# A graph network's last stage: keys and values first, queries behind them in groups of four tiles, biases from a broadcast row, one program block

## Chip, cores and metric

The kernel runs on one core of a Trainium2 chip. The metric is the device time of one execution in microseconds (us); lower is better. A core has five engines with an instruction stream each: TensorE (PE in the profile), VectorE (DVE), ScalarE (ACT), GpSimd (POOL) and SyncE (SP, which here only starts transfers).

## What is computed

The input is 3125 nodes with 128 features and 53125 edges sorted by destination node. Four graph layers follow one another, each with a residual and a layer norm. Three of them sum gathered rows over edges. The fourth, which the change touches with what stands just before it, is an attention over each node's edges:

```python
# h: [3125, 128] after three layers; row = dst, col = src of the edges; 8 heads of 16
x3 = layernorm(x2 + relu(agg @ W.T + b))          # end of layer 3
q = (h @ Wq + bq).reshape(n, 16, 8) * 16 ** -0.5  # h is x3
k = (h @ Wk + bk).reshape(n, 16, 8)
v = (h @ Wv + bv).reshape(n, 16, 8)
s = einsum('edh,edh->eh', q[row], k[col])
p = exp(s - segment_max(s, row)[row])
out = segment_sum(p / segment_sum(p, row)[row] * v[col], row)
```

## The kernel before

Nodes are held in 25 tiles of 128 (`NT`), edges in 416 chunks of 128 (`EC`). Every wait is written by hand: an instruction adds to a semaphore and another engine waits for a count. Each engine works off its own list in order.

The program has two parts, each a block of its own with a meeting of all engines behind it. The first, `sum_layers`, runs three passes over the chunks (the three sum layers), and then a `post_body`, called the bridge below. Each pass gathers its chunks one after another by indirect transfers that POOL issues (L507). At the end of a pass every engine adds one to `s_end`; DVE waits for all four, clears the pass's semaphores and lets the others go on with `s_go` (`pass_end` L371, `pass_close` L1163).

The bridge works tile by tile, in a software pipeline over `i`. For tile t, PE multiplies the summed rows by the layer's weight (`last_product`, L651) and adds the bias by a second, three-row bf16 product (L652); DVE adds the residual and takes the layer norm (`last_front` L1124, L977, L983; `last_back` L987, L1132); PE transposes the normalised tile (L658) and ACT copies it out of PSUM (L728). PE then makes queries, keys and values in one product 384 columns wide (`qkv`, L666) with the bias again as a second product (L667). ACT copies out of PSUM the scaled queries twice, as f32 and as bf16 (L737, L738), and keys and values as f32 (L740). Queries are stored as three bf16 parts whose sum is the f32 value, so DVE takes two differences (`rest`, L1143) and ACT two more casts (`part`, L744) for each tile. SP stores keys and values to `kv_d` in DRAM (L470, three buffers `kv_s`) and queries to `q_d` (L473, six buffers `q_s`). Between them DVE builds tables of penalties for the attention: seven operations at i = 8 (`row_tables`, L1100 to L1110) and 13 pairs from i = 14 (`chunk_tables`, L1116 and L1118). Their data comes by 16 transfers that POOL starts at the head of the bridge into the buffer `G` (L518).

The second part, `attention`, works in 26 steps of 16 chunks, called batches k, each of four quads q (four chunks). POOL gathers the rows of `kv_d` by chunk into `G2` (printed as `G`), a ring of 64 chunks (L1338); before every eighth chunk it waits until the values in that place are used. DVE first clears its buffers, and ACT rewrites the cleared sums (L1536). Then for every quad PE picks out the query rows (L1359, copied out by ACT in L1490, and L1369 into `p_qe`), and DVE multiplies them with the gathered keys (`products`, L1609) and sums by head (L1615). Once in a batch the scores are transposed (PE L1415, into `p_sT`), scanned for segment maxima (DVE L1626), exponentiated on ACT, and turned back. DVE then multiplies values by weights (`values`, L1676, into `PV`), and PE sums them into windows (L1406, L1409, into `p_w`). In most steps one tile of nodes is finished as well: PE L1427, DVE L1709 to L1720, ACT L1531. In `k`'s step DVE runs `products(4k-1)`, `products(4k)`, `products(4k+1)` and `products(4k+2)`, and the step ends with `values(4k-4)` and `values(4k-3)`.

## Time and profile before

| | us |
|---|---|
| median of 3 runs | 2334.08 (2333.65 to 2336.39) |
| the profiled execution | 2332.2 |
| its span | 2330.3 |
| three passes over the chunks | 0 to 1639 |
| the bridge, from its first operation to its last issue of a store | 1639.2 to 1720.2 |
| attention's gathers, first to last start | 1728.6 to 2286.4 |

The busy shares over the span are PE 72%, POOL 70%, DVE 66% and ACT 19%. They are averages over stages that have different limits, so each stage is read from its own rows. The granted TensorE clock was 0.50 of full speed (1.2 GHz) from 1650 to 1700 us, where the bridge runs, and 0.50 from 1750 us on.

### The profile page before, as it was taken

What the parts mean: (1) busy time and instruction counts of PE and PEld (TensorE: products, weight loads), DVE (VectorE), ACT (ScalarE), POOL (GpSimd) and SP (SyncE); (2) the same over time, 40 slices, a digit from 0 to 9 for tenths busy, and PEclk for the clock granted to TensorE, in tenths of its full rate; (3) what the DMA queues carried; (4) which work ended last, traced back from release to release, by engine and by line L of the source; (5) the groups of instructions that cost most, each with busy time, mean ns of one, the idle gap of its engine ahead of it and who ended that gap; (6) DMA issues with size and microseconds to landing.
All of it is one profiled execution on the core that took longest, in us unless ns stands there. A gap on an engine that the chain in (4) does not pass through costs nothing. (4 is left out here: it accounts for less than half of the span.)

```text
span 2330.3 us, 32319 instructions
## 1 busy us (share of the span) xinstructions
PE 1670.3 (72%) x8464; PEld 1238.1 (53%) x8464; DVE 1539.0 (66%) x5260; ACT 435.6 (19%) x994; POOL 1636.8 (70%) x1687
## 2 busy tenths in 40 slices
PE   4877777765766766775567667667957888888886
PEld 3655555553555555554444444444426667677775
DVE  8776776665666666664355555556657787788785
ACT  0000000002000000002111111111343343344342
POOL 6777777775777777775777777774227777777772
PEclk9975555555556665555587777787555555555555
DMA  5233233232233233235232332332423333333331
GB/s 139 56 85 83 57 85 84 56 84 70 56 84 84 85 84 112 56 84 155 54 98 83 98 99 83 98 99 82 80 87 107 105 108 106 108 105 107 108 104 36
DMA packets 149656, 207.12 MB, mean 89 GB/s; under 512 B 48936, under 2 KB 111387, under 8 KB 149360
## 3 DMA queue, kind: packets, MB, share of 16 engines
q0 software_dynamic: 61280, 138.20, 22.1%
q1 hardware_dynamic: 87186, 65.12, 9.5%
q10 hardware_dynamic: 1010, 1.73, 0.2%
q8 instruction: 73, 1.20, 0.2%
q14 instruction: 107, 0.88, 0.1%
HBM read 172.14 MB, written 36.04 MB: 89 GB/s over the span
## 5 line engine op out<-in xcount | busy, mean ns | idle before, releaser
L507 POOL DMA_INDIRECT G<-h_d,idx x832 | 794.6, 955 | 283.9 <-issue 261.8
L570 PE MATMUL p_g<-S,G 128*128 128x96 f32 (+1 forms) x2496 | 609.0, 390 | 462.6 <-DMA G<-h_d,idx 300.7
L570 PEld LDWEIGHTS p_g<-S,G 128*128 128x128 f32 x2496 | 526.6, 292 | 667.2 <-issue 295.0
L1338 POOL DMA_INDIRECT G<-kv_d,idx x416 | 432.4, 1039 | 201.8 <-issue 201.8
L507 POOL DMA_INDIRECT G<-in_x,idx x416 | 397.6, 956 | 132.2 <-issue 119.4
L928 DVE TENSOR_SCALAR work<-iota_h,key_f 128x600 bf16<-128x600 f16 x416 | 171.0, 411 | 253.9 <-PE p_d L581 253.6
L903 DVE SCALAR_TENSOR_TENSOR S<-con,rel,shared 128x96 f32<-128x96 f32 (+1 forms) x1248 | 315.4, 293 | 0.5
L581 PE MATMUL p_d<-work 128*128 128x312 bf16 (+1 forms) x832 | 272.2, 428 | 18.0 <-DVE work L943 17.1
L921 DVE TENSOR_TENSOR agg<-agg,p_g 128x96 f32 (+1 forms) x624 | 143.7, 230 | 104.1 <-PE p_g L570 84.3
L1406 PE MATMUL p_w<-S,PV 128*128 128x40 f32 x832 | 199.2, 415 | 0.7 <-DVE PV L1676 0.7
L943 DVE TENSOR_TENSOR work<-work,p_d 128x312 f32 (+1 forms) x416 | 190.8, 459 | 10.4 <-issue 9.6
L1406 PEld LDWEIGHTS p_w<-S,PV 128*128 128x128 f32 x832 | 186.6, 329 | 15.9 <-issue 10.8
L1019 DVE TENSOR_TENSOR work<-work,p_d 128x512 f32<-128x512 f32 (+1 forms) x168 | 104.3, 625 | 137.1 <-PE p_d L616 136.6
L616 PE MATMUL p_d<-work,q_s 128*128 128x512 bf16 (+1 forms) x525 | 161.0, 429 | 1.9 <-DVE q_s L1008 0.9
L581 PEld LDWEIGHTS p_d<-work 128*128 128x128 bf16 x832 | 116.6, 163 | 34.8 <-DVE work L929 18.1
L1359 PE MATMUL p_oh<-idb,ohn 128*120 128x128 bf16 x416 | 68.9, 321 | 75.8 <-ACT ohn L1483 43.0
L1615 DVE TENSOR_REDUCE hs<-XH 128x32 f32<-128x512 f32 x104 | 111.6, 1073 | 3.5
L705 ACT ACTIVATE xt_s<-p_xt 128x128 f32<-128x128 f32 x75 | 20.8, 278 | 488.8 <-PE p_xt L592 488.8
L929 DVE TENSOR_SCALAR work<-iota_h,lo_f 128x128 bf16<-128x128 f16 x416 | 109.6, 263 | 0.0
L1359 PEld LDWEIGHTS p_oh<-idb,ohn 128*120 128x120 bf16 x416 | 51.9, 213 | 93.0 <-ACT ohn L1483 56.6
L1609 DVE TENSOR_TENSOR XH<-p_qe,G 128x512 f32<-128x512 f32 x104 | 70.8, 681 | 45.7 <-DMA G<-kv_d,idx 35.6
L1676 DVE TENSOR_TENSOR PV<-G,ps 128x512 f32<-128x512 f32 x104 | 68.9, 684 | 20.8 <-PE p_w L1409 20.8
(253 smaller groups left out, 2093.3 us busy)
## 6 DMA issues: line engine op xcount, KB each, us to landing
work<-A_d SPq DMA_DIRECT2D x25, 800.0 KB, 4.5
A_d<-work SPq DMA_DIRECT2D x12, 1600.0 KB, 7.5
G<-h_d,idx POOLq DMA_INDIRECT x832, 2.5
G<-in_x,idx POOLq DMA_INDIRECT x416, 2.5
G<-kv_d,idx POOLq DMA_INDIRECT x416, 2.8
h_d<-XH SPq DMA_DIRECT2D x75, 64.0 KB
h_d<-in_x SPq DMA_DIRECT2D x2, 1600.0 KB, 7.4
kv_d<-kv_s SPq DMA_DIRECT2D x25, 128.0 KB, 1.7
```

What stands on the lines that cost most here:

```text
L507: pool.indirect_dma_start(G[:, c % GRING, :], None, l.table, bass.IndirectOffsetOnAxis(ap=l.places[:, c:c + 1], axis=0)).then_inc(s_arr[g ...
L570: last = pe.matmul(p_g[:, g % PB, 0:width], G[:, c % GRING, :], S[:, c % (SRING * GR), 0:width], start=(k == 0), stop=(k == GR - 1))
L581: last = pe.matmul(p_d[:, 1 + half, 0:(hi - lo) * W], lows[:, slot, :], keys[:, slot, lo * W:hi * W], start=(k == 0), stop=(k == GR - 1))
L616: last = pe.matmul(p_d[:, n % 3, 0:width], q_s[:, t % QS, k, :], A_s[:, t % AB, cols], start=(k == 0), stop=(k == QR - 1))
L903: last = dve.scalar_tensor_tensor(S[:, slot + k, 0:l.nb * W].rearrange("p (b w) -> p b w", w=W), bc(iota, 1, l.nb), rel[:, c:c + 1], bc(co ...
L921: dve.tensor_tensor(place, place, p_g[:, g % PB, 0:l.nb * W].rearrange("p (b w) -> p b w", w=W), ALU.add).then_inc(s_added, 1)
L928: dve.tensor_scalar(keys[:, slot, :], iota_h[:], key_f[:, c:c + 1], None, ALU.is_equal)
L943: dve.tensor_tensor(place, place, p_d[:, 1 + half, 0:(hi - lo) * W].rearrange("p (t w) -> p t w", w=W), ALU.add).then_inc(s_bad, 1)
L1338: pool.indirect_dma_start(G[:, c % KRING, :], None, d["kv"], bass.IndirectOffsetOnAxis(ap=idx[:, c:c + 1], axis=0)).then_inc(s_ar[c // QC ...
L1359: last = pe.matmul(p_oh[0:QR * WA, c * P:(c + 1) * P], ohn[:, k % 2, j * QC + c, :], idb[:], start=True, stop=True)
L1406: pe.matmul(p_w[:, q % 2, 0:WA], PV[:, q % 2, c, :], S01[:, j * QC + c, :], start=(c == 0), stop=(c == QC - 1))
L1615: dve.tensor_reduce(hs[:, j * QC:(j + 1) * QC, :], prod[:, j * QC:(j + 1) * QC, :].rearrange("p c (d h) -> p c h d", h=HEADS), AX_X, ALU.a ...
```

## The change

- Keys and values are made on their own, 256 columns wide. DVE takes them out of PSUM and adds the bias, which lies as a row broadcast over all partitions (`b_all`). The two bias products are gone, and the bias split that made their operands.
- The transposed tiles are kept in `H`. When all keys and values are done, PE makes the queries out of them, four tiles in one PSUM bank (seven groups, the last of one tile). DVE scales and adds the bias, and the three parts are made for four tiles at once; a store takes one group.
- The seven row tables are spread over i = 3 to 9, and the chunk tables begin at i = 10 instead of 14.
- There is one block instead of two. POOL does not meet the others at the end of the bridge: it waits for the stores of keys and values and for the tables, adds its one to `s_end`, and starts on attention's gathers. `agg` and `G` are placed first, so that `G2` lies over these two alone.

The diff without its changes of indentation (all four engine functions are moved from the blocks into plain functions); "..." marks what is left out:

```diff
-QS = 6
+QS = 3
+QG = 4
+QGROUPS = math.ceil(NT / QG)
...
+            def _(pool):
+                sums.gpsimd(pool)
+                att.gpsimd(pool)
...
+            def _(dve):
+                att.vector(dve, sums.vector(dve))
...
@@ SP @@
             def post_body():
-                for i in range(NT + 4):
-                    if i < NT:
-                        sp.wait_ge(s_kv, i + 1)
-                        sp.dma_start(d["kv"][i * P:(i + 1) * P, :], kv_s[:, i % 3, :]).then_inc(s_kvst[i % 3], 16)
-                    if (t := i - 4) >= 0:
-                        sp.wait_ge(s_q[4], t + 1)
-                        sp.dma_start(d["q"][t * P:(t + 1) * P, :],
-                                     q_s[:, t % QS].rearrange("p s d -> p (s d)")).then_inc(s_qst[t % QS], 16)
+            for t in range(NT):
+                sp.wait_ge(s_kv, t + 1)
+                sp.dma_start(d["kv"][t * P:(t + 1) * P, :], kv_s[:, t % 3, :]).then_inc(s_kvst[t % 3], 16)
+            for g in range(QGROUPS):
...
+                sp.wait_ge(s_q[5], g + 1)
+                sp.dma_start(rows, q_p[:, g % 3, 0:n].rearrange("p t s d -> p t (s d)")).then_inc(s_qst[g % 3], 16)
...
@@ POOL @@
             post_body()
-            pass_end(pool, turn)
+        for k in range(3):
+            pool.wait_ge(s_kvst[k], 16 * len(range(k, NT, 3)))
+        pool.wait_ge(s_tab, 7 + KB)
+        pool.sem_inc(s_end, 1)
...
@@ PE @@
             def last_product(t):
-                pe.matmul(p_g[:, t % 3, 0:D], aggT[:, t * P:(t + 1) * P], w_lin[:], start=True, stop=False)
-                pe.matmul(p_g[:, t % 3, 0:D], one_three[:], b_three[:, 0:D], start=False, stop=True).then_inc(s_o, 1)
+            pe.matmul(p_g[:, t % 3, 0:D], aggT[:, t * P:(t + 1) * P], w_lin[:], start=True, stop=True).then_inc(s_o, 1)
...
-                pe.matmul(p_d[:, t % 3, 0:3 * D], xt_s[:, t % 2, :], w_qkv[:], start=True, stop=False)
-                pe.matmul(p_d[:, t % 3, 0:3 * D], one_three[:], b_three[:, D:4 * D], start=False,
-                          stop=True).then_inc(s_qkv, 1)
+            pe.matmul(p_d[:, t % 3, 0:2 * D], H[:, t, :], w_qkv[:, D:3 * D], start=True, stop=True).then_inc(s_pkv, 1)
+
+        def queries(g):
+            if g < 3:
+                pe.wait_ge(s_kv, NT - 2 + g)
+            else:
+                pe.wait_ge(s_q[0], g - 2)
+            for j in range(min(QG, NT - g * QG)):
+                last = pe.matmul(p_d[:, (NT + g) % 3, j * D:(j + 1) * D], H[:, g * QG + j, :], w_qkv[:, 0:D],
+                                 start=True, stop=True)
+            last.then_inc(s_pq, 1)
...
@@ ACT @@
+        def part(g, k):
+            n = min(QG, NT - g * QG)
+            act.wait_ge(s_q[2 * k], g + 1)
...
+            act.activation(q_p[:, g % 3, 0:n, k, :], q_f[:, g % 3, 0:n, :], ACT.Copy).then_inc(s_q[2 * k + 1], 1)
...
@@ DVE @@
             def last_front(t):
-                dve.scalar_tensor_tensor(y[:, t % 2, :], p_g[:, t % 3, 0:D], 0.0, XA[:, t, :], ALU.max,
-                                         ALU.add).then_inc(s_y, 1)
+            dve.tensor_tensor(y[:, t % 2, :], p_g[:, t % 3, 0:D], b_lin, ALU.add).then_inc(s_y0, 1)
+            dve.wait_ge(s_y0, t + 1)
+            dve.scalar_tensor_tensor(y[:, t % 2, :], y[:, t % 2, :], 0.0, XA[:, t, :], ALU.max, ALU.add).then_inc(s_y, 1)
...
+        def keys_values(t):
+            dve.wait_ge(s_pkv, t + 1)
+            if t >= 3:
+                dve.wait_ge(s_kvst[t % 3], 16 * (t // 3))
+            dve.tensor_tensor(kv_s[:, t % 3, :], p_d[:, t % 3, 0:2 * D], b_kv, ALU.add).then_inc(s_kv, 1)
+
+        def scaled(g):
...
+            dve.scalar_tensor_tensor(q_f[:, g % 3, 0:n, :], p_d[:, (NT + g) % 3, 0:n * D].rearrange("p (t d) -> p t d", d=D),
+                                     float(HD) ** -0.5, bc(b_q, 1, n), ALU.mult, ALU.add).then_inc(s_q[0], 1)
...
+            dve.tensor_tensor(part, part, q_p[:, g % 3, 0:n, k - 1, :], ALU.subtract).then_inc(s_q[2 * k], 1)
...
             def post_body():
-                for i in range(NT + 6):
+            for i in range(NT + 4):
...
+                    keys_values(i - 4)
+                if 3 <= i < 10:
+                    row_tables(i - 3)
+                if 10 <= i < 10 + KB // 2:
+                    chunk_tables(i - 10)
+            dve.wait_ge(s_bq, 1)
+            for i in range(QGROUPS + 2):
+                if i < QGROUPS:
+                    scaled(i)
+                for k in (1, 2):
+                    if 0 <= i - k < QGROUPS:
+                        rest(i - k, k)
```

POOL's list from the last of the bridge's transfers to attention's gathers, before:

```order
L518 DMA G<-in_flat 8x26x130 x16
L372 REGISTER_ALU
L391 UNCONDITIONAL_BRANCH
L1328 UNCONDITIONAL_BRANCH
L1332 TENSOR_LOAD ns_i
L1332 ISA x2
L1284 UNCONDITIONAL_BRANCH
L1338 DMA G<-kv_d,idx 128x256 x416
```

and in the changed kernel (L540 is the old L518, L1365 the old L1338):

```order
L540 DMA G<-in_flat 8x26x130 x16
L1359 TENSOR_LOAD ns_i
L1359 ISA x2
L1315 UNCONDITIONAL_BRANCH
L1365 DMA G<-kv_d,idx 128x256 x416
```

The register step of `pass_end` and the two branches from block to block are gone between the transfers and the gathers; the waits in their place are the ones in the diff.

DVE's list for one tile of the bridge with a chunk table, before (L1124 to L983 are `last_front`, L987 and L1132 `last_back`, L1143 `rest`, L1116 and L1118 the table):

```order
L1124 SCALAR_TENSOR_TENSOR y<-p_g,XH 128x128
L977 BN_STATS bn6<-y 128x6
L983 BN_AGGR mv<-bn6 128x2
L1143 TENSOR_TENSOR q_r<-q_r,q_s 128x128
L987 RECIPROCAL rstd<-std 128x1
L1132 ISA
L1132 TENSOR_SCALAR XH<-y,mv,rstd 128x128
L1143 TENSOR_TENSOR q_r<-q_f,q_s 128x128
L1116 TENSOR_TENSOR shared<-G 128x258
L1118 TENSOR_SCALAR shared<-shared 128x258
```

and in the changed kernel:

```order
L1138 TENSOR_TENSOR y<-p_g,b_all 128x128
L1140 SCALAR_TENSOR_TENSOR y<-y,XH 128x128
L993 BN_STATS bn6<-y 128x6
L999 BN_AGGR mv<-bn6 128x2
L1003 RECIPROCAL rstd<-std 128x1
L1147 ISA
L1147 TENSOR_SCALAR XH<-y,mv,rstd 128x128
L1155 TENSOR_TENSOR kv_s<-p_d,b_all 128x256
L1130 TENSOR_TENSOR shared<-G 128x258
L1132 TENSOR_SCALAR shared<-shared 128x258
```

Both differences of the query parts left the tile; an addition of the bias at its head and the copy of keys and values came in.

## Rows read from the trace of the kernel before

**Rows 1.** Section 4 of the page: the chain that ended last, shares by engine.

```profile
POOL 19%; issue 6%; PE 1%; DVE 0%; DMA 0%; ACT 0%; DVEq 0%; POOLq 0%
```

**Rows 2.** Timeline of POOL (start us, duration us, engine, line, operation, idle before).

```profile
1642.94 10.33 POOL L518 DMA_DIRECT2D G<-in_flat  x16 [1.57 <-issue]
...
1728.65 1.04 POOL L1338 DMA_INDIRECT G<-kv_d,idx  x1 [75.38 <-issue]
```

**Rows 3.** Timeline of PE, one tile of the bridge.

```profile
1691.24 1.49 PE L666 MATMUL p_d<-w_qkv,xt_s 128*128 128x384 f32 x2
1692.66 0.50 PE L667 MATMUL p_d<-b_three,one_three 3*128 3x384 bf16 x1
1693.09 0.80 PE L651 MATMUL p_g<-w_lin,work 128*128 128x128 f32 x2
1693.82 0.28 PE L652 MATMUL p_g<-b_three,one_three 3*128 3x128 bf16 x1
```

**Rows 4.** Timeline of DVE, one tile of the bridge with a chunk table.

```profile
1691.09 0.29 DVE L1124 SCALAR_TENSOR_TENSOR y<-p_g,XH 128x128 f32<-128x128 f32 x1 [0.59 <-PE p_g L652]
1691.41 0.29 DVE L977 BATCH_NORM_STATS2 bn<-y 128x6 f32<-128x128 f32 x1
...
1691.84 0.27 DVE L1143 TENSOR_TENSOR q_r<-q_r,q_s 128x128 f32<-128x128 f32 x1
1692.03 0.16 DVE L987 RECIPROCAL rstd<-std 128x1 f32<-128x1 f32 x1
...
1694.14 0.29 DVE L1124 SCALAR_TENSOR_TENSOR y<-p_g,XH 128x128 f32<-128x128 f32 x1 [0.59 <-PE p_g L652]
```

**Rows 5.** Line L518, the 16 transfers for the tables: from issue to landing.

```profile
DMA to landing us min/median/max: 5.0/9.1/13.0
```

**Rows 6.** Section 6 of the page: stores of keys and values (us to landing last).

```profile
kv_d<-kv_s SPq DMA_DIRECT2D x25, 128.0 KB, 1.7
```

**Rows 7.** Timeline of ACT in the bridge, the copy of the fifth tile.

```profile
1661.13 0.28 ACT L737 ACTIVATE q_f<-p_d 128x128 f32<-128x128 f32 x1 [3.51 <-PE p_d L667]
```

**Rows 8.** Timeline from the last query stores to the first product of attention.

```profile
1717.83 2.37 SPq L473 DMA_DIRECT2D q_d<-q_s  x5
...
1727.25 0.23 DVE L1567 CAST idb<-con 128x128 bf16<-128x128 f32 x1 [8.70 <-PEq L391]
...
1751.80 0.69 DVE L1609 TENSOR_TENSOR XH<-p_qe,G 128x512 f32<-128x512 f32 x1 [9.45 <-PE p_qe L1369]
```

**Rows 9.** Waits of the SP queue, 1600 to 1760 us (us in total, times, longest).

```profile
SPq L391 <- PEq L391: 4.9, 1, 4.9
```

**Rows 10.** Waits in the whole of attention, 1750 to 2331 us.

```profile
DVE XH L1609 <- DMA G<-kv_d,idx: 35.6, 46, 2.4
```

**Rows 11.** Waits of DVE from 1779 to 1811 us.

```profile
DVE XH L1609 <- DMA G<-kv_d,idx: 5.8, 4, 2.4
```

**Rows 12.** Waits of DVE from 1972 to 1984 us.

```profile
DVE XH L1609 <- DMA G<-kv_d,idx: 3.1, 2, 2.4
```

**Rows 13.** Timeline of PE and DVE over one step of attention that finishes a tile.

```profile
2001.66 0.68 PE L1359 MATMUL p_oh<-idb,ohn 128*120 128x128 bf16 x4 [1.82 <-ACT ohn L1483]
...
2007.77 0.65 PE L1359 MATMUL p_oh<-idb,ohn 128*120 128x128 bf16 x4 [0.78 <-ACT oht L1490]
2009.08 1.93 PE L1406 MATMUL p_w<-S,PV 128*128 128x40 f32 x8
...
2008.76 0.69 DVE L1609 TENSOR_TENSOR XH<-p_qe,G 128x512 f32<-128x512 f32 x1 [1.03 <-DMA G<-kv_d,idx]
...
2014.58 0.42 DVE L1626 TENSOR_TENSOR_SCAN FB<-shared,p_sT 128x128 f32<-128x128 f32 x1 [1.63 <-PE p_sT L1415]
...
2023.32 0.68 PE L1359 MATMUL p_oh<-idb,ohn 128*120 128x128 bf16 x4 [1.82 <-ACT ohn L1483]
```

**Rows 14.** Timeline of POOL and DVE in the same step.

```profile
2007.05 1.50 POOL L1338 DMA_INDIRECT G<-kv_d,idx  x1 [0.30 <-issue]
...
2006.45 1.28 DVE L1676 TENSOR_TENSOR PV<-G,ps 128x512 f32<-128x512 f32 x2
```

More of the change, by code:

```diff
@@ L1 @@
 import math
+from collections import namedtuple
 from contextlib import ExitStack
@@ L178, in program, with _ @@
         cont = sb("cont", [P, KB])
+        s_arr = [ctx.enter_context(nc.semaphore(f"s_arr{k}")) for k in range(GP)]
         with ExitStack() as mid:
-            sum_layers(nc, mid, a, d, con, dst_s, base4, n_f, ns_i, XH, idx, shared, cont)
-        attention(nc, ctx, out, d, con, dst_s, base4, ns_i, XH, idx, shared, cont)
+            sums = sum_layers(nc, mid, a, d, con, dst_s, base4, n_f, ns_i, XH, idx, shared, cont, s_arr)
+        att = attention(nc, ctx, out, d, con, dst_s, base4, ns_i, XH, idx, shared, cont, s_arr)
+        with nc.Block() as block:
+            @block.sync
+            def _(sp):
+                sums.sync(sp)
+                att.sync(sp)
+            @block.gpsimd
+            def _(pool):
+                sums.gpsimd(pool)
+                att.gpsimd(pool)
+            @block.tensor
+            def _(pe):
+                sums.tensor(pe)
+                att.tensor(pe)
+            @block.scalar
+            def _(act):
+                sums.scalar(act)
+                att.scalar(act)
+            @block.vector
+            def _(dve):
+                att.vector(dve, sums.vector(dve))
 class Layer:
@@ L328, in sum_layers @@
     s_fill = sem("s_fill")
-    s_qkv, s_kv, s_st = sem("s_qkv"), sem("s_kv"), sem("s_st")
-    s_q = [sem(f"s_q{k}") for k in range(5)]
+    s_pkv, s_kv, s_st, s_pq = sem("s_pkv"), sem("s_kv"), sem("s_st"), sem("s_pq")
+    s_q = [sem(f"s_q{k}") for k in range(6)]
     s_kvst = [sem(f"s_kvst{k}") for k in range(3)]
@@ L1185, in _ @@
                 pass_close()
-            post_body()
+        with dve.Fori(0, iterations(dve)):
+            iteration_start()
+            sums_body(L[2])
+            dve.wait_ge(s_da, len(DENSE))
             pass_close()
-def attention(nc, ctx, out, d, con, dst_s, base4, ns_i, XH, idx, shared, cont):
+        gathered = dve.alloc_register("gathered_dve")
+        dve.reg_mov(gathered, turn)
+        post_body()
+        pass_close()
+        return gathered
+    return Engines(sync, gpsimd, tensor, scalar, vector)
@@ L1191, in sb, with attention @@
+def attention(nc, ctx, out, d, con, dst_s, base4, ns_i, XH, idx, shared, cont, s_arr):
     def sb(name, shape, dt=F32):
@@ L1265, in attention @@
     s_end, s_go = sem("s_end2"), sem("s_go2")
-    s_ar = [sem(f"s_ar{k}") for k in range(KQ)]
     def p_po(t):
@@ new lines, in sync, with window, store, body @@
+    def sync(sp):
+        turn = sp.alloc_register("turn2_sp")
+        sp.reg_mov(turn, 0)
+        ns = sp.value_load(ns_i[0:1, 0:1], min_val=1, max_val=NSW)
+        regs = [sp.alloc_register(f"qoff{k}") for k in range(QRING)]
+        def window(q):
+            if q % QRING == 0:
+                sp.load(regs, q_off[0:1, q:q + QRING])
+            off = sp.snap(regs[q % QRING], min_val=0, max_val=NP)
+            if q >= QRING:
+                sp.wait_ge(s_qe, q - QRING + 1)
+            sp.dma_start(QW[:, q % QRING, :], d["q"][bass.ds(off, WA), :].rearrange("n (s d) -> (n s) d", s=QR)).then_inc(s_qw[q % QRING], 16)
+        def store(t):
+            rows = min(N - t * P, P)
+            sp.wait_ge(s_done, t + 1)
+            sp.dma_start(out[t * P:t * P + rows, :], o_s[0:rows, t % OR, :]).then_inc(s_os[t % OR], 16)
+        def body():
+            sp.wait_ge(s_lay, 2)
+            for k in range(-2, KB + 3):
+                if batch(k + 2):
+                    for j in range(4):
+                        window((k + 2) * 4 + j)
+                for t in in_step(k - 1):
+                    store(t)
+            for k in range(OR):
+                sp.wait_ge(s_os[k], 16 * len(range(k, NT, OR)))
+        passes(sp, ns, turn, body)
@@ new lines, in gpsimd, with body @@
+    def gpsimd(pool):
+        turn = pool.alloc_register("turn2_pool")
+        pool.reg_mov(turn, 0)
+        ns = pool.value_load(ns_i[0:1, 0:1], min_val=1, max_val=NSW)
+        def body():
+            for c in range(EC):
+                if c >= KRING and c % (2 * QC) == 0:
+                    pool.wait_ge(s_pv, (c - KRING) // QC + 2)
+                pool.indirect_dma_start(G[:, c % KRING, :], None, d["kv"],
+                                        bass.IndirectOffsetOnAxis(ap=idx[:, c:c + 1], axis=0)
+                                        ).then_inc(s_arr[c // QC % KQ], 16)
+        passes(pool, ns, turn, body)
@@ L1787, in layout @@
+    return Engines(sync, gpsimd, tensor, scalar, vector)
 def layout(i):
```

2236 lines of the change are left out of this document (1075 added, 1161 removed).

## The prediction

> **What bounds the kernel now.** I began with the chain that ended last. It follows POOL's gathers back through the whole of attention [rows 1], and by that view whatever starts the gathers sooner is worth its full size. The chain stops where those gathers start, so the next view was POOL's timeline: after the tables' transfers, issued from 1642.94 to 1653.3 us, POOL is idle 75.4 us until the first gather at 1728.65 [rows 2]. That is the bridge, and the change starts the gathers inside it.
>
> In the bridge PE never rests. One tile takes 3.05 us from one DVE `L1124` to the next, and DVE waits 0.59 us of it for PE [rows 4]. PE's share by start-to-start times: the product for queries, keys and values 1.42, its bias 0.43, the layer's product 0.73 with its bias behind it [rows 3].
>
> Then the third view, which decides: are the gathers really what attention waits for? DVE waits 35.6 us for them in 46 places [rows 10]. But look at what follows such a wait. In a step that finishes a tile, DVE's product at 2008.76 has waited 1.03 us for a gather, and the scan behind it, at 2014.58, waits another 1.63 us, for PE. PE reaches its window sums (2009.08, two runs of them stand before `p_sT`) not late because of DVE, but behind a run of L1359 at 2007.77 that waited for ACT's copy [rows 13]. Without the gather's wait DVE would only wait that much longer for PE. From 2001.66 to the same run of L1359 at 2023.32 the step takes 21.66 us, and going from one to the other through PE, `p_sT`, DVE's scan, ACT and PE again, I find no gather on the way. So in these steps, most of the 26, attention runs at its own pace. It is different where no tile is finished: from 1779 to 1811 DVE waits 5.8 us for gathers in 4 places, the longest 2.4 [rows 11], from 1972 to 1984 3.1 us in 2 [rows 12], and behind these the scan does not wait for PE. Together 8.9 us.
>
> Why do gathers keep exactly the pace of the steps, if they do not set it? The first gather of attention took 1.04 us [rows 2]; the one at 2007.05 takes 1.50 beside DVE's two `PV` products, 2006.45 to 2007.73, and ends 0.8 us behind them [rows 14]. A gather that comes to the same DVE operation in every step is held to the step's rhythm. By the Trainium skill (SBUF — State Buffer, "SBUF: two separate sides") GpSimd and VectorE share a port pair as a lock, so a transfer issued by GpSimd stands until VectorE's operation ends; the stretched gather agrees. By that rule gathers follow DVE and an earlier start pays only where DVE really waited; by the chain of rows 1 alone it would pay in full.
>
> **The change part by part.**
>
> *Keys and values.* PE loses the two bias products and a third of the 1.42 us. DVE loses two differences, 0.19 us from start to start each [rows 4], and gains the bias addition (like `L1124`, 0.32 to the dependent operation behind it) and the copy of 256 columns. No row shows that copy: it lies between 0.19 (128 columns) and 0.73 (512 columns out of PSUM, the 0.69 us operation of rows 8 with its gap); I take 0.35, a third of the way. DVE's tile with a chunk table: 3.05 - 0.59 - 0.38 + 0.32 + 0.35 = 2.75, and as its last operation now overlaps the next tile, 2.7 us. PE's: 3.05 - 0.43 - 0.47 - 0.2 (L652's 0.28 less its overlap) = 1.95. DVE becomes the bound, so the gain per tile is 0.35 us, not 1.1. Tiles without tables take about 2.0.
>
> *The head of the bridge.* It cannot be fast. The tables' transfers land 5.0 to 13.0 us after issue [rows 5], the last one thus by 1653 + 13 = 1666, and the tables at i = 10 wait for them. While they run, stores of keys and values are late too: the fifth tile's copy on ACT waited 3.5 us, for one of three buffers [rows 7]. DVE alone would be at i = 10 by about 1661 (ten tiles at 2.1); with both waits I put it at 1667. This wait is new on DVE, and everything is behind it.
>
> *Sum to the gathers.* 1667 + 13 x 2.7 = 1702; two tiles at 2.0: 1706; the last norm, transpose, copy, product and addition about 2.7: 1709; landing 1.7 [rows 6]; POOL's way to its first gather about 1.4 (as from 1727.25 to 1728.65, rows 8 and 2): 1712. That is 17 us sooner than 1728.65.
>
> *Queries.* They now come after. PE needs 25 products, each between 0.47 (a third of 1.42) and 0.73 us [rows 3]: 12 to 18 us. I take 0.47, since here they stand one behind another as in the wide product. DVE has three passes over 512 columns for six groups, at about 0.6 us: 11. From 1709, two for the first group, 12, and three rounds for the last group's parts (about 3): stored at 1726, landed 1727.5 at the latest. Before, the last store was issued at 1720.2 [rows 8].
>
> *One block.* The meeting behind the first block cost SP a wait of 4.9 us [rows 9]; it is gone, and DVE goes from its `pass_close` straight to L1567. So attention's compute starts at about 1726.7 against 1727.25 [rows 8]: the queries eat what the meeting gives, gain 0.5 us. With 0.73 per product it is a loss of 6, with a fast head of the bridge a gain of 4. From there to the first product, 24.55 us [rows 8], nothing changes, and no gather is waited for in it.
>
> *Attention.* The gathers are 17 us ahead, so the waits of rows 11 and 12 go: 8.9. The other 26.7 us of waits become waits for PE, worth 0; a few tenths come back at the last gather. The lead of some 13 chunks fits into the ring of 64, and POOL's waits for room do not begin.
>
> The bias split and the broadcast load stand ahead of the first two passes' sums, while POOL's gathers, which need neither, already run; 0, and 2 us if that cover failed.
>
> Sum: 0.5 + 8.9 + 0.1 = 9.5 us. The span goes from 2330.3 to 2320.8, the profiled execution from 2332.2 to 2322.7. The median of the runs was 1.9 above the profiled execution: 2334.1 - 9.5 = 2324.6.
>
> **Rivals.**
> - *Gathers set the pace everywhere.* For it: rows 1 and the wait in nearly every step. Against it: the wait for PE behind each. All of the lead would pay: 2334.1 - 17 = 2317. Chance 0.18.
> - *Queries end late.* Products at 0.73 us, or a slow hand-over through three buffers and six rounds between DVE and ACT: attention starts 6 us later, gains 8.9: 2331, no change to be measured. Chance 0.12.
> - *Slower.* The bridge's query part decides: if each of the seven groups took 4 us (PE 2.9, and then three DVE and three ACT passes not overlapped), it would end at 1709 + 28 + 3 = 1740, attention would start 15 us late and regain 8.9: 2340. It decides from 4 us a group on (the point of no gain is 3 us). DVE's order, with its two differences behind the next scaled group, speaks against. Chance 0.06.
> - *The gathers' start does not come forward*, since the last tile's store or the tables are late: only the start of attention counts, 2333 to 2334. Chance 0.04.
>
> **How the numbers follow.** My case has 0.60, with its own range 2320 to 2329. What a measurement here can tell from no change is 0.2%, 4.7 us. Faster: 0.60 and 0.18, and a part of the second rival, 0.82. Within 0.2%: 0.11. Slower: 0.07. The range reaches down to the first rival with an early start of attention, 2313, and up to the second, 2331.
>
> **What the changed profile would show.** POOL's first gather of `kv_d` at 1712 (1706 to 1716), DVE without a wait for PE in most tiles of the bridge, a DVE wait of some us for the transfers near 1660. L1567's successor at 1727 (1722 to 1733). DVE's wait for gathers in attention near 0, and its wait for `p_sT` and `p_w` up by some 20 us: if instead the steps shrink to 20.5 us, the first rival is right. The steps that held the waits of rows 11 and 12 shorter by about 3 us each. I am wrong, too, if the ACT and PE rounds of these steps are slowed by gathers beside the bridge's last passes.

## The result, and the profile after

The changed kernel takes 2339.35 us (median of 19 runs, 2336.50 to 2344.03), the kernel before 2334.28 (19 runs beside them). The ratio is 1.0022, 95% interval 1.0015 to 1.0028: about 5 us slower, where 9.5 us faster was predicted. The profiled span is 2336.1 us, against 2330.3.

The runs whose names begin with e, f and h fell on executions in which the engines stand still again and again (in the profiles of e1, f1 and h1 all of them together at 58 to 62 places for 1.5 to 6 us, in that of the changed kernel here at 4 places for up to 3) and in which the kernel before takes 2979 to 3033 us, so their ratios hold for that condition only, and of them I use the profiles of the bridge and of the first 20 us, which look as elsewhere.

In what follows, "answers to [rows n]" means that the lines show in the changed kernel what that group of rows shows in the kernel before. The chain that ended last, by engine (page, section 4), answers to [rows 1]:

```profile
POOL 41%; PE 21%; issue 17%; DVE 9%; DMA 8%; ACT 3%; DVEq 0%; ACTq 0%; POOLq 0%; SPq 0%
```

The chain no longer stops at the bridge: it runs to the layers. POOL's timeline answers to [rows 2]:

```profile
1645.46 10.15 POOL L540 DMA_DIRECT2D G<-in_flat  x16 [1.57 <-issue]
1715.31 1.05 POOL L1365 DMA_INDIRECT G<-kv_d,idx  x1 [59.70 <-issue]
```

The first gather starts 13.3 us sooner than the 1728.65 of before. But the whole bridge begins 2.5 us later here (1642.18 against 1639.67 for its first transfer), so within the bridge the gain is 15.9 us. One tile with a chunk table on VectorE, and the two waits that precede these tiles, answer to [rows 4] and [rows 7]:

```profile
1662.76 0.42 DVE L1155 TENSOR_TENSOR kv_s<-p_d,b_all 128x256 f32<-128x256 f32 x1 [4.29 <-DMA kv_d<-kv_s]
1667.53 0.43 DVE L1155 TENSOR_TENSOR kv_s<-p_d,b_all 128x256 f32<-128x256 f32 x1 [2.46 <-DMA kv_d<-kv_s]
...
1690.31 0.42 DVE L1155 TENSOR_TENSOR kv_s<-p_d,b_all 128x256 f32<-128x256 f32 x1
1690.65 0.42 DVE L1130 TENSOR_TENSOR shared<-G 128x258 f32<-128x258 int32 x1
...
1692.92 0.42 DVE L1155 TENSOR_TENSOR kv_s<-p_d,b_all 128x256 f32<-128x256 f32 x1
```

From 1690.31 to 1692.92 a tile takes 2.61 us, with no wait for TensorE, and the copy of 256 columns is worth 0.34 us start to start. Then the queries, from the last copy of keys and values (1711.53) to the cast of the identity matrix with which attention begins (1742.51, called the ident cast below); VectorE, ScalarE and SP's stores:

```profile
1711.53 0.42 DVE L1155 TENSOR_TENSOR kv_s<-p_d,b_all 128x256 f32<-128x256 f32 x1 [0.43 <-PE p_d L685]
1713.31 0.69 DVE L1162 SCALAR_TENSOR_TENSOR work<-p_d,b_all 128x512 f32<-128x512 f32 x1 [1.35 <-PE p_d L693]
...
1718.52 20.25 SPq L502 DMA_DIRECT2D q_d<-work  x7
...
1721.60 1.67 ACT L762 ACTIVATE work<-work 128x512 bf16<-128x512 f32 x3 [3.10 <-DMA q_d<-work]
1723.37 0.69 DVE L1162 SCALAR_TENSOR_TENSOR work<-p_d,b_all 128x512 f32<-128x512 f32 x1 [2.88 <-ACT work L762]
...
1726.13 1.67 ACT L762 ACTIVATE work<-work 128x512 bf16<-128x512 f32 x3 [2.87 <-DMA q_d<-work]
...
1730.87 1.67 ACT L762 ACTIVATE work<-work 128x512 bf16<-128x512 f32 x3 [3.07 <-DMA q_d<-work]
...
1735.52 2.41 ACT L762 ACTIVATE work<-work 128x128 bf16<-128x128 f32 x6 [2.98 <-DMA q_d<-work]
...
1742.51 0.43 DVE L1591 CAST idb<-con 128x128 bf16<-128x128 f32 x1 [5.12 <-SPq L403]
```

Read ScalarE's four rows from the fourth group on: each burst of three passes takes 1.67 us, and ahead of each ScalarE waits about 3 us for a store. The groups follow each other every 4.5 to 4.7 us. The line of the stores gives the other half:

```profile
L502 SPq DMA_DIRECT2D q_d<-work x7: 372/372/578, 1718.5 to 1738.2; - x7
...
DMA to landing us min/median/max: 2.8/3.0/3.9
```

So the ident cast comes at 1742.51 in place of 1727.25 [rows 8]: 15.3 us later. What stands just ahead of it differs too. At the end of its first block the kernel before has this on POOL (line L391, from the view of that line):

```profile
L391 POOLq DRAIN  x1: 4723/4723/4723, 1722.2 to 1722.2; - x1
```

SP's waits for the query stores are over at 1721.6 there, and the other four engines reach the block's end at 1722.2 to 1722.3; POOL, which had to meet them first, is in its drain until 1727.0, and the ident cast follows at 1727.25. The changed kernel has no such drain, and its last query store, issued at 1738.19, lands 0.6 us ahead of the ident cast.

From the ident cast to the end of the span the kernel before needs 603.05 us, the changed one 593.6. VectorE's waits in attention answer to [rows 10]:

```profile
DVE PV L1700 <- PE p_w L1435: 48.6, 25, 2.2
DVE FB L1650 <- PE p_sT L1441: 32.9, 23, 1.7
```

No wait for gathers is left, and the step that finishes a tile keeps its pace, answering to [rows 13]:

```profile
2008.23 0.69 PE L1385 MATMUL p_oh<-idb,ohn 128*120 128x128 bf16 x4 [1.82 <-ACT ohn L1508]
...
2029.88 0.68 PE L1385 MATMUL p_oh<-idb,ohn 128*120 128x128 bf16 x4 [1.82 <-ACT ohn L1508]
```

21.65 us, before 21.66. The steps that held the waits of [rows 11] and [rows 12] are shorter. One of them, from its first product to the first product of the next step (timeline of VectorE), before:

```profile
1798.32 0.69 DVE L1609 TENSOR_TENSOR XH<-p_qe,G 128x512 f32<-128x512 f32 x1 [0.17 <-PE p_qe L1369]
...
1820.60 0.67 DVE L1609 TENSOR_TENSOR XH<-p_qe,G 128x512 f32<-128x512 f32 x1
```

and in the changed kernel:

```profile
1811.41 0.67 DVE L1633 TENSOR_TENSOR XH<-p_qe,G 128x512 f32<-128x512 f32 x1
...
1830.48 0.67 DVE L1633 TENSOR_TENSOR XH<-p_qe,G 128x512 f32<-128x512 f32 x1
```

22.28 us against 19.07. Counted in the same way, the step just before it takes 20.36 against 18.13 us, and the one from 1971.30 on 22.28 against 19.06; the other steps agree within 0.1 us.

The account of the two profiles: 2.5 (the layers) + 12.8 (the bridge, from its first transfer to the ident cast: 100.3 us in place of 87.6) - 9.5 (attention) = 5.8 us, the difference of the spans.

The 2.5 us begin in the first 20 us, where one gather is held. Timeline of POOL and VectorE:

```profile
9.16 5.45 DVE L802 MEMSET agg<- 128x6464 f32 x1 [1.30 <-issue]
...
10.50 5.36 POOL L529 DMA_INDIRECT G<-in_x,idx  x1 [0.30 <-issue]
16.17 0.95 POOL L529 DMA_INDIRECT G<-in_x,idx  x1 [0.30 <-issue]
```

Most of the gathers around it take 0.94 us; in the kernel before none of the first 20 us is longer than 1.79. By 19.1 us the kernel before has started its eleventh gather, the changed one its seventh (18.67). By the Trainium skill (SBUF — State Buffer, "SBUF: two separate sides") a transfer that GpSimd issues stands still while VectorE holds the ports that the two share, and VectorE takes them for an operation in a 2-port mode or with two SBUF inputs. The 5.36 us look like a transfer held in this way, but a memset has no input, and the same memset stands in the kernel before and holds none.

### The profile page after: what moved, and what is told of

It is laid out like the page before. It is cut to its first block, busy times and chain, and to the rows that moved or that the text cites. A ratio compares the mean times of both kernels' runs of the same rounds, so it can differ in the third digit from the quotient of the medians.

```text
span 2336.1 us, 32097 instructions
## 1 busy us (share of the span) xinstructions
PE 1630.6 (70%) x8440; PEld 1237.9 (53%) x8464; DVE 1551.0 (66%) x5276; ACT 418.9 (18%) x891; POOL 1636.3 (70%) x1687
## 4 chain that ended last, share of the span: by engine, by line
POOL 41%; PE 21%; issue 17%; DVE 9%; DMA 8%; ACT 3%; DVEq 0%; ACTq 0%; POOLq 0%; SPq 0%
POOL G L529 41%; PE p_w L1432 6%; PE p_g L594 4%; DMA G<-h_d,idx 3%; DMA G<-in_x,idx 3%; PE p_oh L1385 2%; PE p_w L1435 2%; DVE hs L1639 1%; PE p_d L640 1%; DVE XH L1633 1%; PE p_o L625 1%; PE p_d L605 1%; ACT oht L1515 1%; DMA q_d<-work 1%; DMA kv_d<-kv_s 1%
## 5 line engine op out<-in xcount | busy, mean ns | idle before, releaser
L1365 POOL DMA_INDIRECT G<-kv_d,idx x416 | 430.0, 1034 | 186.1 <-issue 185.8
L605 PE MATMUL p_d<-work 128*128 128x312 bf16 (+1 forms) x832 | 268.7, 423 | 23.7 <-DVE work L959 22.7
L1432 PEld LDWEIGHTS p_w<-S,PV 128*128 128x128 f32 x832 | 186.6, 329 | 15.9 <-issue 10.8
L640 PE MATMUL p_d<-work,q_s 128*128 128x512 bf16 (+1 forms) x501 | 151.1, 420 | 6.7 <-issue 4.3
L734 ACT ACTIVATE xt_s<-p_xt 128x128 f32<-128x128 f32 x75 | 20.8, 277 | 486.1 <-PE p_xt L616 486.1
L1700 DVE TENSOR_TENSOR PV<-G,ps 128x512 f32<-128x512 f32 x104 | 69.0, 684 | 48.6 <-PE p_w L1435 48.6
L640 PEld LDWEIGHTS p_d<-work,q_s 128*128 128x128 bf16 x525 | 60.4, 124 | 38.6 <-issue 15.3
```

Of the source, the lines that this page charges most:

```text
L605: last = pe.matmul(p_d[:, 1 + half, 0:(hi - lo) * W], lows[:, slot, :], keys[:, slot, lo * W:hi * W], start=(k == 0), stop=(k == GR - 1))
L640: last = pe.matmul(p_d[:, n % 3, 0:width], q_s[:, t % QS, k, :], A_s[:, t % AB, cols], start=(k == 0), stop=(k == QR - 1))
L1365: pool.indirect_dma_start(G[:, c % KRING, :], None, d["kv"], bass.IndirectOffsetOnAxis(ap=idx[:, c:c + 1], axis=0)).then_inc(s_arr[c // QC ...
L1432: pe.matmul(p_w[:, q % 2, 0:WA], PV[:, q % 2, c, :], S01[:, j * QC + c, :], start=(c == 0), stop=(c == QC - 1))
```

## The experiments

**e1, seven buffers for the query parts.** The edit (cut; "..." marks what is left out, and all uses of `q_p` and `s_qst` follow):

```
+QB = 7
-    q_p = work[:, w_3:w_3 + 3 * QG * QR * D // 2] ... g=3
+    q_p = work[:, w_3:w_3 + QB * QG * QR * D // 2] ... g=QB
-            if k == 0 and g >= 3:
-                act.wait_ge(s_qst[g % 3], 16 * (g // 3))
+            if k == 0 and g >= QB:
+                act.wait_ge(s_qst[g % QB], 16 * (g // QB))
```

> The changed kernel with seven buffers for the grouped queries' parts in place of three, so that no group waits for a store. Theory A (latency): with three buffers each group from the fourth on begins only when the store of three groups before has landed, 3.0 us after an issue that itself follows the last pass of that group, so every group takes 1.5 us of ACT work plus 3.0 us of landing = 4.6 us. Then the ACT waits for query stores (12.0 us, 4 times) vanish, the ident cast comes near 1730 in place of 1742.5, and the kernel takes 12 to 13 us less than the changed kernel: about 2327 us, 0.3% below the kernel before. Theory B (contention: the gathers that now begin at 1715 slow the stores) and theory C (the stores' own throughput, 384 KB each): seven stores still take their 4.6 us each one after the other, the final wait of SP takes the place of the waits on ACT, and at most 3 us are gained: about 2336 us.

**e2, four buffers** (`QB = 4`).

> The changed kernel with four buffers for the parts in place of three. Theory A: a group waits for the store of four groups before, which was issued one group of ACT work earlier, so the landing is shared by two groups: (3.1 + 1.5) / 2 = 2.3 us per group in place of 4.6, waits only from the fifth group on; 3 waited groups at 2.3 plus one free group: 9 to 11 us sooner than the changed kernel, about 2329 us. Theories B and C: one more buffer lets one group go ahead and changes nothing of the pace of 4.6 us: the last store lands as late as before, 0 to 1.5 us gained, about 2338 us.

**e3, the gathers held back.** In POOL, ahead of attention:

```
         pool.wait_ge(s_tab, 7 + KB)
+        for k in range(QS):
+            pool.wait_ge(s_qst[k], 16 * len(range(k, QGROUPS, QS)))
```

> The changed kernel, but the first attention gather waits until all query stores have landed. Theory A: query groups keep their pace of 4.6 us and the landing its 3.0 us, since gathers have no part in it; the first gather then comes after the ident cast, as in the kernel before, and the 9.5 us that attention was shorter are lost: 2339 + 9.5 = about 2348 us. Theory B (gathers slow the stores): landings fall from 3.0 to 2 us or less, groups take 3.5 us, the queries end 4 to 5 us sooner, so about 2344 us. Rival on the gain: if attention is not shorter because of the lead of the gathers but for another reason (order of SBUF tensors, clock), the time stays near 2339.

**e4, the bias load later**: the `dma_start` into `b_all` moves behind `npass = loops(act)`.

> The changed kernel, but the load of the biases into all partitions (256 KB, issued at 4.90 in the burst of loads at the start) is issued only after the pass count is known, near 18 us. In the profile of the changed kernel the fourth gather took 5.36 us in place of 0.94 while that load was under way, and each later pass began 2.5 to 3.7 us later than before. Theory D: the load in the burst delays the gathers: the long gather vanishes, the passes begin where they did in the kernel before, 2.3 to 3 us less than the changed kernel: about 2336.7 us. Rival: the place of agg and G in SBUF, or one profile's chance: no difference, 2339 us.

Ratios to the kernel before in that condition: e1 0.9961 (0.9944 to 0.9979), e2 0.9951 (0.9931 to 0.9970), e3 1.0026 (1.0011 to 1.0042), e4 0.9961 (0.9941 to 0.9980). From the last key and value copy to the ident cast e1 takes 22.7 us, e2 23.0, e3 28.2, e4 (the change's own query stage) 31.4. So the seven buffers took about 8 us out of the bridge where I expected 12 to 13, and e1 and e4, 8.8 us apart there, have the same ratio: in that condition the times do not resolve such a difference. Four buffers are as good as seven, since with four a store has one more group's time to land. The wait of e2's ScalarE for stores (us, times):

```profile
  DMA q_d<-work: 0.8, 1
```

That is theory A's mechanism, a landing that stands in series, though my 2.3 us per group in e2 came out as 2.65, for another reason (see l1). Theories B and C, by which the stores themselves keep 4.6 us a group, fall: the groups of e1 and e2 follow each other every 2.65 us. A little of B is true: with the gathers held the median landing is 2.6 us, with them 3.0 to 3.3 in e1, e2 and the changed kernel. e4 has the long gather all the same (4.42 us, ending at 15.87), so theory D falls.

**f1, the changed kernel as it is; f2, as e1; f3, as e3; f4, the kernel before with `agg` and `G` declared first.**

> The changed kernel as it is, beside the other three on one chip. The runs before this one ran on a chip on which the kernel before takes 2983 us, 28% more, with stalls of 20 to 40 us in every engine, and there the changed kernel was not among them. Theory A (latency of the stores plus a late start of the layers): 0.2% over the kernel before again, 2339 us where that takes 2334.

> Seven buffers for the query parts, as in e1. From e1's profile the stretch from the last key and value copy to the ident cast is 22.7 us in place of 31.0 us in the changed kernel. Theory A, with the size that e1 showed (no waits for stores, 2.2 us for a group): 8.3 us less than the changed kernel, 2331 us, 0.14% below the kernel before. Rival: the gain of the attention shrinks because the lead of the gathers is 8 us shorter (they begin 19 us before the ident cast in place of 27): then 2334 us or more.

> Gathers held until the query stores have landed, as in e3. In e3's profile the landing of a query store was 2.6 us in place of 3.0 to 3.3, and the stretch from the last key and value copy to the ident cast 28.2 us in place of 31.0 (31.5 in e4). If the 9.5 us that the attention is shorter come from the lead of the gathers, this gives the changed kernel's time + 9.5 - 2.8: 2346 us. If the attention keeps its gain without the lead: 2336.5 us.

> The kernel before with one part of the change alone: agg and G are declared first in the layers' SBUF, in place of behind the query tiles. In all five profiles with that order one of the first gathers took until 15.86 to 15.87 us (4.3 to 5.9 us long, even where the load of the biases was moved out of the burst); in the kernel before none did. Theory D2 (place in SBUF): the long gather appears here too, the first gather of the second pass starts near 548.9 in place of 545.2, and the kernel takes 2 to 3 us more than before: 2336.8 us. Rival (the load's DMA or other parts of the change do it): no long gather, 2334.3 us.

Measured: f1 0.9973 (0.9949 to 0.9997), f2 0.9968 (0.9947 to 0.9990), f3 1.0047 (1.0029 to 1.0066), f4 1.0000 (0.9978 to 1.0022). In that condition the changed kernel is a little faster than before, so the sign of this change is no property of the kernel alone. f1 and f2 are not told apart. f3 lies 23 us over f1, more than the 7 expected; perhaps the lead of the gathers is worth more where engines stall, which no run tests. f4 has no long gather (the longest that starts in the first 18 us takes 1.46), so the place in SBUF is not its cause.

**g2, the accumulator cleared in eight memsets**, in the changed kernel:

```
-        dve.memset(agg[:, 0:2, :], 0.0).then_inc(s_part, 1)
+        flat_agg = agg[:, 0:2, :].rearrange("p b n -> p (b n)")
+        for k in range(8):
+            part = dve.memset(flat_agg[:, k * AGW // 4:(k + 1) * AGW // 4], 0.0)
+        part.then_inc(s_part, 1)
```

> The changed kernel, but VectorE clears the sums' accumulator at the start in eight memsets of a quarter plane in place of one of 5.45 us. f4 showed that the place of agg and G does not make the long gather, and e4 that the load of the biases does not. In the six profiles with the long gather it ends at 15.86 or 15.87 us, which is the end of this memset (14.61) + 0.31 + 0.94, so theory D3: the gather is held until the memset's end. Then in this kernel a gather is held at most for the rest of one piece: none of the first ten takes over 2 us, and the second pass starts 2 to 3 us sooner than with the one memset. Rival (something else ends at 15.86): a gather of 4 to 6 us that ends at 15.86 again.

One run: 2337.14 us beside 2335.12 of the kernel before, too few to tell a difference. The longest early gather, with the memsets:

```profile
7.98 6.67 DVE L804 MEMSET agg<- 128x808 f32 x8
...
14.12 1.79 POOL L529 DMA_INDIRECT G<-in_x,idx  x1 [0.30 <-issue]
```

Theory D3 holds: the length of that memset makes the length of the hold. The second pass began at 545.88 in place of 548.87.

**h1 to h3: seven buffers; gathers held; seven buffers with eight memsets.**

> Seven buffers for the query parts, as in e1 and f2, for a chip on which the kernel before takes 2334 us as in the first comparison. Theory A: the stretch from the last key and value copy to the ident cast is 22.7 us in place of 31.0, and nothing later changes, so 8.3 us less than the changed kernel: 2331 us, ratio 0.9986 to the kernel before. Rival (the attention's gain shrinks with the lead of the gathers, 19 in place of 27 us): 2334 us or more, ratio 1.000.

> Gathers held until the query stores have landed, as in e3 and f3, for the same chip. Landings 2.6 us in place of 3.0, so the queries end 2.8 us sooner; if the 9.5 us by which the attention is shorter come from the lead of the gathers: 2339.3 + 9.5 - 2.8 = 2346 us, ratio 1.005. If the attention keeps its gain without the lead: 2336.5 us, ratio 1.001.

> Seven buffers for the query parts, and the accumulator cleared in eight memsets (g2: no long gather; the second pass began 3.0 us, the third 1.5 and the bridge 1.2 us sooner than in the changed kernel). Both together: 8.3 + 1.2 us less than the changed kernel: 2330 us, ratio 0.998 to the kernel before. Rival: the head start of the layers is taken up by waits that follow, and this is h1's time.

Ratios 0.9932 (0.9905 to 0.9958), 1.0034 (1.0009 to 1.0059), 0.9937 (0.9914 to 0.9961): the signs and the order of e and f again, h1 and h3 not told apart; nothing on the sizes for the usual condition.

**k1, seven buffers; k2, gathers held,** now with the kernel before at 2333.84 us.

> Seven buffers for the query parts, for the undisturbed chip. Theory A: 8.3 us less than the changed kernel, 2331 us, ratio 0.9986. Rival (the attention's gain shrinks with the shorter lead of the gathers): ratio 1.000 or more.

> Gathers held until the query stores have landed, for the undisturbed chip. If the lead of the gathers is what shortens the attention by 9.5 us: 2346 us, ratio 1.005. If not: 2336.5 us, ratio 1.001.

k1: 2331.35 us, ratio 0.9988 (0.9979 to 0.9997). k2: 2346.60 us, ratio 1.0053 (1.0039 to 1.0066). Both as theory A has them, to 0.6 us. k1's timeline of VectorE, and its ident cast:

```profile
1719.93 0.69 DVE L1163 SCALAR_TENSOR_TENSOR work<-p_d,b_all 128x512 f32<-128x512 f32 x1 [0.77 <-ACT work L763]
1720.54 1.28 DVE L1170 TENSOR_TENSOR work<-work 128x512 f32<-128x512 f32 x2
1722.58 0.69 DVE L1163 SCALAR_TENSOR_TENSOR work<-p_d,b_all 128x512 f32<-128x512 f32 x1 [0.77 <-ACT work L763]
...
1735.86 0.23 DVE L1592 CAST idb<-con 128x128 bf16<-128x128 f32 x1 [5.28 <-SPq L404]
```

k2's first gather (POOL's timeline) comes behind its ident cast:

```profile
1743.39 1.04 POOL L1367 DMA_INDIRECT G<-kv_d,idx  x1 [86.53 <-issue]
```

and in its attention the waits for gathers of [rows 10] are back:

```profile
DVE XH L1635 <- DMA G<-kv_d,idx: 34.1, 43, 2.4
```

**l1, four buffers for the full-precision groups on top of k1; l2, l1 with eight memsets; l3, the changed kernel in two blocks.**

```
-    w_3 = 3 * QG * D
+    w_3 = 4 * QG * D
-            if g >= 3:
-                dve.wait_ge(s_q[5], g - 2)
+            if g >= 4:
+                dve.wait_ge(s_q[5], g - 3)
```

(and `q_f[:, g % 4, ...]`); for l3 `sums.sync` to `sums.vector` stand in one `nc.Block()`, `att.sync` to `att.vector` in a second.

> As k1 (seven buffers for the query parts), and four buffers in place of three for the full-precision groups, so that VectorE's pass on group g no longer waits for ScalarE's last pass on group g-3. In k1's profile VectorE waits 3.1 us in four such waits, and a group takes 2.15 us where its three VectorE passes take 0.69 + 0.60 + 0.60 = 1.9. Theory A: 2 to 3 us less than k1: 2329 us, ratio 0.9977. Rival: ScalarE's three passes of 0.63 and its waits for VectorE set the pace: the wait moves to ScalarE, under 1 us gained, 2331 us.

> As l1, and the accumulator cleared at the start in eight memsets (g2). Theory: the gathers of the first 16 us are not held and the layers end 1.2 us sooner, as in g2's profile: l1's time less 1.2 us: 2328 us, ratio 0.997. Rival: the head start is used up by waits that follow: l1's time.

> The changed kernel, but with a block for the layers and one for the attention, as before the change; so the gathers begin after the block's end on every engine. Theory: the one block is worth nothing by itself beside the early gathers: k2's time, 2346 to 2347 us, ratio 1.0053, and the long gather of the start is there all the same. Rival (my prediction's term: a barrier of 4.9 us goes with the second block): 4 to 5 us over k2: 2351 us, ratio 1.0073.

l1: 2330.57 us beside 2336.49, ratio 0.9977 (0.9968 to 0.9986). This interval and k1's overlap, so what l1 gains over k1 is read from the two profiles alone. VectorE's groups in l1 have no gap left:

```profile
1720.20 0.68 DVE L1163 SCALAR_TENSOR_TENSOR work<-p_d,b_all 128x512 f32<-128x512 f32 x1
1720.80 1.28 DVE L1170 TENSOR_TENSOR work<-work 128x512 f32<-128x512 f32 x2
1722.01 0.68 DVE L1163 SCALAR_TENSOR_TENSOR work<-p_d,b_all 128x512 f32<-128x512 f32 x1
...
1734.51 0.23 DVE L1592 CAST idb<-con 128x128 bf16<-128x128 f32 x1 [6.23 <-SPq L404]
```

A group takes 1.81 us in place of k1's 2.65, but the last store then takes 4.9 us to land, and VectorE's closing wait grows from 5.28 to 6.23, so of the 0.84 x 4 = 3.4 us saved the bridge keeps 2.2 (last copy to ident cast 20.4 us against k1's 22.7).

l2: 2324.71 us, ratio 0.9949 (0.9936 to 0.9963), the fastest of all and 11.8 us below the kernel before. The memsets gave 5.9 us over l1, where 1.2 were expected; the two intervals allow about 3 to 10. h1 and h3, which differ in the same way, were not told apart. l3: 2349.83 us, ratio 1.0055 (1.0042 to 1.0069), k2's ratio; the rival's 1.0073 lies outside. Its ident cast waits 4.92 us, k2's 4.88:

```profile
1740.59 0.23 DVE L1579 CAST idb<-con 128x128 bf16<-128x128 f32 x1 [4.92 <-PEq L190]
```

Yet l3 is no test of what the block's end cost in the kernel before. It has the same drain on POOL, but early, since its POOL does not meet the others at the end of the bridge (view of line L190):

```profile
L190 POOLq DRAIN  x1: 4723/4723/4723, 1714.7 to 1714.7; - x1
```

It runs from 1714.7 to 1719.4, beside the queries, and is over 20 us before the other engines get there. In the three profiles with the old bridge (before, f4, m2) the same 4.72 us stand between the last store's landing and the ident cast.

**m2, the kernel before with eight memsets.**

> The kernel before with the accumulator cleared in eight memsets, as in g2 and l2. In l2 that was worth 5.9 us over l1, more than the 1.2 us of g2's profile. In the two profiles of before's form (before, f4) no gather is held by the one memset. Theory (the pieces only undo the held gather that the change brought): no difference, 2334 us, ratio 1.000. Rival (they help by themselves, through the order of the first loads or the place of later work): 2 to 5 us less than before, ratio 0.998 to 0.9990, and then half or more of what l2 gains over before has nothing to do with the change.

Ratio 0.9996 (0.9987 to 1.0005): no difference is seen, and one of more than 3 us is excluded. So most of what the pieces win in l2 belongs to the change.

The places of the bridge side by side (us, one profile each; "first transfer" is POOL's first in the bridge, "tail" is ident cast to end of span):

| kernel | first transfer | last copy | first gather | ident cast | tail | ratio |
|---|---|---|---|---|---|---|
| before | 1639.67 | | 1728.65 | 1727.25 | 603.05 | 1 |
| m2 | 1642.16 | | 1733.45 | 1732.06 | 603.5 | 0.9996 |
| after | 1642.18 | 1711.5 | 1715.31 | 1742.51 | 593.6 | 1.0022 |
| g2 | 1640.96 | 1709.5 | 1713.27 | 1741.28 | 594.0 | one run |
| k1 | 1643.32 | 1713.2 | 1716.97 | 1735.86 | 593.6 | 0.9988 |
| k2 | 1643.44 | 1713.2 | 1743.39 | 1742.39 | 603.1 | 1.0053 |
| l1 | 1645.12 | 1714.1 | 1717.84 | 1734.51 | 594.2 | 0.9977 |
| l2 | 1637.82 | 1706.9 | 1710.63 | 1725.79 | 594.3 | 0.9949 |
| l3 | 1643.22 | 1712.4 | 1741.99 | 1740.59 | 603.7 | 1.0055 |

## Why the prediction was wrong, step by step

*Keys and values: right.* 2.61 us a tile against 2.7, VectorE the bound, the copy 0.34 against 0.35. *Head of the bridge:* right in kind, mis-sized. VectorE waits for the landing of stores of keys and values alone (4.29 and 2.46), never for the tables' transfers, for which I had forecast a wait near 1660. The first chunk table comes at 1672.40, within the bridge 2.9 us later than the predicted 1667; the faster tiles behind it made it good. *Sum to the gathers: right, with the help of luck.* From the bridge's first transfer to the last copy 69.35 us, by my sum 1709 - 1639.67 = 69.3, because the late head and the faster tiles cancel; to the first gather 73.1 against 72.3.

*Queries: the step that failed.* I wrote of "three passes over 512 columns for six groups, at about 0.6 us: 11", stored at 1726, and let attention start at 1726.7, 17.7 us behind the last copy. It was 31.0. VectorE's passes had the duration that I gave them (0.6 start to start). The products were cheaper. Two instructions make one product; in the view of their line by stretches, TensorE's granted clock stands behind the busy times of PE and PEld:

```profile
1711.50:1713.50 2.00, 2.00 (x11) 2.00 (x11) 0.50 0.38 131
1715.00:1717.00 2.00, 2.00 (x20) 2.00 (x20) 1.00 0.00 0
```

A product took 0.43 us start to start at the low clock (0.50, 1.2 GHz) until 1714, near my 0.47, and 0.22 at the full clock (1.00, 2.4 GHz) from 1714.3 on; TensorE had been busy without a gap since 1708.2 when the clock rose. All 24 took 6.93 us.

What I left out was the ring of buffers. Group g may overwrite its parts only when the store of group g-3 has landed; that store is issued behind the last pass of g-3, which is done in the round before g's. Landing (3.0 us) and ScalarE's round (1.67) therefore add up, 4.6 us a group, on four groups. I had named "a slow hand-over through three buffers" and priced it at 6 us, and 4 us per group as the case that makes it slower, and gave them 0.12 and 0.06, with passes that do not overlap as the reason; the store's landing stood in neither. That slower case said 2340 with attention 15 us late, and 2339.35 and 15.3 were measured: the price was right and the reason was not.

The last store's landing was missing as well: I let attention start 0.7 us behind its issue, earlier even than my own landing time of 1727.5. The overrun of 13.3 us divides by the profiles: 8.3 the waits for stores (after against k1), 2.2 VectorE's wait of 0.77 us per group for ScalarE's last pass, also a ring of three (k1 against l1), and 2.8 left. In these, l1's last store to ident cast is 5.5 us where I allowed 0.7, against products and passes that were 2 us shorter than my sum.

*One block: the 4.9 us are gone, as I said, but they were not what I took them for.* In the kernel before they are POOL's drain of 4.72 us at the block's end, with the last store already landed; the view of the waits [rows 9] puts them down to PE. In the changed kernel VectorE waits 5.12 us ahead of the ident cast all the same, and this wait is for the last store's landing, which is the term missing above. What takes the drain off the path is that POOL no longer meets the others there: l3 has two blocks, its drain runs beside the queries, and it takes as long as k2 with one block.

*Attention: right, and the largest claim against the chain view.* 9.5 us against 8.9 and a few tenths, and at the places named: the two steps with the waits of [rows 11] give 2.2 and 3.2 us (5.8 predicted), the one with [rows 12] 3.2 (3.1 predicted), all other steps up to the last together 0.2, and the last step with the end 0.6. k2 shows that it is the gathers' lead: without it the tail is 603.1 again. And the full lead does not pay: it is 27.2 us in the changed kernel, 18.9 in k1 and 15.2 in l2, and the tail is 593.6, 593.6 and 594.3. VectorE's 35.6 us of waits for gathers became 29.0 us more of waits for TensorE (48.6 + 32.9 against 20.8 + 31.7), as the step with [rows 13] said.

*The layers: predicted 0, "2 us if that cover failed".* The size is near, the cause was not the biases. In the profiles k1, k2, l1, l3 and after, with the held gather, the bridge begins at 1642.2 to 1645.1, mean 1643.5; in before, g2, l2 and m2, without it, at 1637.8 to 1642.2, mean 1640.2: 3.3 us. But these are single profiles, and m2 without a held gather begins its bridge where the changed kernel does (1642.16 and 1642.18), so the 2.5 us between the two profiles cannot be put down to the gather alone; the timed pair l1 and l2 gives it 5.9 us, about 3 to 10. That the long memset in the changed kernel holds the gather is shown (g2, h3 and l2 against the other profiles). Why the same memset holds none in the kernel before stays open. The bias load (e4), the place of the tiles (f4) and the one block (l3, which has a gather of 4.05 us) are excluded. One guess fits all profiles: in the changed kernel the operation queued behind the memset has two SBUF inputs (`rel`), in the kernel before a small memset of `one_three` stood between them and is gone. By the Trainium skill (the same page, "Who interferes with whom") a VectorE operation with two SBUF inputs contends with a GpSimd operation that reads SBUF, and the gather's indices lie there; yet the page also says that a `tensor_tensor` did not stall such a transfer in its own probe. Whether VectorE takes the ports already while the memset ahead still runs, no run here tested.

So the profiles add up to 2.5 (layers) + 12.8 (bridge) - 9.5 (attention) = 5.8 us, and the timed difference is 5.1. Behind the 12.8 stand the two rings and the last landing, set against the drain that is gone; even with both rings opened (l1) the bridge takes 89.4 us against 87.6. The 2.5 are within what single profiles scatter.

## What to carry to other kernels

When work is cut into groups that go round a ring of buffers, write the cycle out: buffer free after store landed, store issued after the last pass, last pass a round later. If the landing is in that cycle once with no round to spare, it counts in full for every group; one more buffer took 8 us out of the bridge here. Add the landing of the last store, too, which nothing hides. A wait at a block's end should be traced in the view of that line, engine by engine: the 4.9 us here were one engine's drain, and moving that engine's meeting was enough to take them off the path, with one block or two. And waits "for gathers" on an engine are worth only what the next wait behind them does not take over: 9.5 of 35.6 us here, whatever the lead from 15 to 27 us.

## What the runs showed of the hardware

- A gather issued by POOL beside one memset of 5.45 us can stand until the memset's end (all 14 profiles of the changed layers that keep the one memset, 3.79 to 5.86 us long in place of 0.94, ending 1.25 us behind it), and with eight memsets over the same columns none of the first 20 us exceeds 1.95 us (g2, h3, l2). In the kernel before, f4 and m2 none is held.
- The median landing of a store of 384 KB was 2.6 us with no gathers beside it (e3, k2, l3) and 3.0 to 3.4 with them (after, e1, e2, g2, k1, l1); where stores were issued every 1.8 us (l1) in place of 2.65 (k1) the longest took 4.9 in place of 4.1.
- A drain of POOL at the end of a block took 4.72 us in each of the four profiles that have one behind the bridge (before, f4, l3, m2), and in l3, where it ran beside the queries, no engine waited for it.
- Products of 128 x 128 x 128 in fp32 one behind another took 0.43 us each at a granted clock of 0.50 and 0.22 at 1.00 (24 in 6.93 us), where a third of the wide product at 0.50 had given 0.47.
